# Attention sums in a fused conv, attention and expert kernel: both key blocks multiplied with the ones on TensorE, in place of one product of their GpSimd sum

## The reference

```python
dots = jnp.einsum('bhid,bhjd->bhij', q, k) * scale
attn = jax.nn.softmax(dots, axis=-1)
out = jnp.einsum('bhij,bhjd->bhid', attn, v)
```

## Time and profile before

| | |
|---|---|
| median of 3 runs | 1380.11 us |
| the profiled execution | 1380.82 us, its span 1378.8 us |
| TensorE matmul, busy in the span | 1135.6 us (82%) |
| VectorE | 827.9 us (60%) |
| ScalarE | 627.5 us (46%) |
| GpSimd | 573.8 us (42%) |
| L626, GpSimd's additions | 128 of 2360 ns |
| L1117, the products with the ones | 1024 passes, 83.5 us busy |

### The profile page before, as it was taken

One profiled execution on the slowest core, in us unless ns is written; L12 is line 12 of the kernel. 1 busy time (PEld: TensorE's weight loads), 2 busy tenths in 40 slices (PEclk: granted clock), 3 DMA queues, 4 the chain that ended last, 5 costly groups with the idle time before them and its releaser, 6 DMA issues.

```text
span 1378.8 us, 29094 instructions
## 1 busy us (share of the span) xinstructions
PE 1135.6 (82%) x10071; PEld 739.4 (54%) x10071; DVE 827.9 (60%) x1478; ACT 627.5 (46%) x1113; POOL 573.8 (42%) x437
## 2 busy tenths in 40 slices
PE   3989897966699989897987992149999999999943
PEld 2444444433244544453444442139899999998732
DVE  1556554665688768877787664525555555555545
ACT  0646455643477568557655761023333333333411
POOL 1414132333388658688877885221111221112100
PEclk9999999987699989999999997569999999999975
DMA  3124293635032221322324122921111121111258
GB/s 106 62 94 166 77 391 110 196 90 179 16 75 73 73 71 50 111 78 79 89 80 116 33 70 74 369 83 47 48 47 47 47 58 51 48 47 44 67 161 308
DMA packets 96376, 138.93 MB, mean 101 GB/s; under 512 B 18152, under 2 KB 71464, under 8 KB 95496
## 3 DMA queue, kind: packets, MB, share of 16 engines
q1 hardware_dynamic: 85032, 94.39, 22.9%
q0 software_dynamic: 11232, 42.94, 8.8%
HBM read 83.55 MB, written 53.56 MB: 99 GB/s over the span
## 4 chain that ended last, share of the span: by engine, by line
PE 65%; DVE 13%; DMA 6%; issue 5%; POOL 3%; ACT 3%; DVEq 2%; SPq 2%; PEldq 0%; ACTq 0%; POOLq 0%; PEld 0%
PE PP L894 22%; PE PP L1234 13%; PE PP L1109 7%; PE PP L1128 6%; DVE mxp L1430 5%; PE PP L962 3%; PE PP L1117 3%; PE PP L1050 3%; PE PP L928 3%; PE PP L1008 3%; POOL list_d L658 2%; DMA list_d<-WORK,idx 1%; PE PP L1207 1%; DVEq L1435 1%; DMA WORK<-in_L_ffn_W_dram 1%
## 5 line engine op out<-in xcount | busy, mean ns | idle before, releaser
L1430 DVE TENSOR_REDUCE mxp<-PP 128x2 f32<-128x1024 f32 x256 | 301.2, 1218 | 87.0 <-PE PP L1050 86.6
L834 ACT ACTIVATE WB<-PP 128x512 f32<-128x512 f32 x512 | 269.6, 604 | 175.2 <-PE PP L1128 174.6
L626 POOL TENSOR_TENSOR WB<-WB 128x1024 f32<-128x1024 f32 x128 | 301.5, 2360 | 105.8 <-PE PP L1117 95.2
L866 ACT ACTIVATE WORK<-PP,b1c 128x256 f32<-128x256 f32 (+1 forms) x320 | 143.7, 450 | 257.4 <-PE PP L894 253.9
L709 POOL DMA_INDIRECT y_d<-WORK,place x71 | 73.1, 1030 | 347.0 <-DVE WORK L1758 337.5
L894 PE MATMUL PP<-WORK,WB 128*128 128x256 f16 (+1 forms) x1920 | 208.0, 264 | 3.1 <-DVE WORK L1733 3.0
L1234 PE MATMUL PP<-WB,WORK 128*128 x1704 | 193.9, 273 | 0.0
L894 PEld LDWEIGHTS PP<-WORK,WB 128*128 x1920 | 176.8, 99 | 29.5 <-issue 4.0
L1128 PE MATMUL PP<-WORK 97*128 97x256 f16 x1024 | 162.5, 283 | 23.8 <-ACT WB L834 20.0
L1234 PEld LDWEIGHTS PP<-WB,WORK 128*128 128x128 f16 x1704 | 164.5, 98 | 21.0 <-issue 0.4
L605 POOL TENSOR_TENSOR WB<-WORK,WB 128x1024 f16<-128x1024 f32 x32 | 67.9, 2122 | 222.1 <-ACT WORK L746 222.0
(11 more groups left out here) (236 smaller groups left out, 1097.9 us busy)
## 6 DMA issues: line engine op xcount, KB each, us to landing
WORK<-in_L_ffn_W_dram POOLq DMA_DIRECT2D x32, 512.0 KB, 4.2
WORK<-list_d SPq DMA_DIRECT2D x32, 258.0 KB, 2.9
res_d<-WORK SPq DMA_DIRECT2D x8, 1024.0 KB, 4.6
WB<-late_d SPq DMA_DIRECT2D x4, 2048.0 KB, 15.9
WORK<-y_d SPq DMA_DIRECT2D x16, 512.0 KB, 8.8
WORK<-in_x_dram SPq DMA_DIRECT2D x8, 512.0 KB, 4.0
v_d<-WORK SPq DMA_DIRECT2D x4, 1024.0 KB, 5.4
WORK<-q_hi_d SPq DMA_DIRECT2D x16, 256.0 KB, 3.8
```

Source lines behind the costliest of these rows:

```text
L626: pool.tensor_tensor(PS[n % 2], PR[n % 3][:, 0], PR[n % 3][:, 1], ALU.add).then_inc(s("pair_kept"), 1)
L834: act.activation(PR[n % 3][:, c // 2, c % 2 * 2:c % 2 * 2 + 2], SCORES[m % 3] .rearrange("p (h n) -> p h n", h=2), ACT.Exp).then_inc(s("e_ ...
L866: act.activation(hid[u][:, k, 0:width], hidden_bank(k)[:, 0:width], ACT.Gelu, bias=b1c[:, bass.ds(e, 1), k], scale=1.0 / WSCALE)\
L1430: dve.tensor_reduce(mxp[:, n // 4 % 2, i, h:h + 2, k], PP[2 + h // 2][:, :].rearrange("p (h n) -> p h n", h=2), X_AXIS, ALU.max).then_inc( ...
```

## The change

The GpSimd no longer adds the two key blocks, and the buffers `PS` and the semaphore `pair_kept` are gone. In their place `sum_heads` multiplies each of the two blocks' exponentials with the ones, in 8 float32 products and so 16 passes a step, which accumulate in the same place. It needs no wait of its own, since `weigh_heads` just ahead of it has waited for the same exponentials. GpSimd keeps the wait for `pv_made` at the head of each step of its loop.

```diff
-        PS = [WB[:, e].bitcast(F32)[:, 12 * QN:16 * QN].rearrange("p (h n) -> p h n", h=GH) for e in (E - 3, E - 4)]
...
-            def add_pair(n):
-
-                pool.wait_ge(s("e_kept"), 4 * n + 4)
-                if n >= 2:
-                    pool.wait_ge(s("pv_made"), FREE + n - 1)
-                pool.tensor_tensor(PS[n % 2], PR[n % 3][:, 0], PR[n % 3][:, 1], ALU.add).then_inc(s("pair_kept"), 1)
...
             for n in range(B * STEPS):
                 b, t = n // STEPS, n % STEPS
-                add_pair(n)
+                pool.wait_ge(s("pv_made"), FREE + n - 1) if n >= 2 else None
...
-                pe.wait_ge(s("pair_kept"), n + 1)
-                for h in range(GH):
-                    mm = pe.matmul(WEIGHED[h * D:(h + 1) * D, QN:2 * QN], onesf[:, :], PS[n % 2][:, h],
-                                   start=False, stop=(n % 4 == 3), skip_group_check=True)
+                for i in range(2):
+                    for h in range(GH):
+                        mm = pe.matmul(WEIGHED[h * D:(h + 1) * D, QN:2 * QN], onesf[:, :], PR[n % 3][:, i, h],
+                                       start=False, stop=(n % 4 == 3 and i == 1), skip_group_check=True)
```

More of the change, by code:

```diff
@@ L289, in hybrid_block @@
                      "ld_stage0 ld_stage1 scaled split_hi split_lo st_last wts_split "
-                     "ld_g0 ld_g1 ld_m0 ld_m1 sum_kept rin_kept rstd_kept ld_nm mx_made mx_kept pair_kept ld_sum inv_kept st_inv ld_inv0 ld_inv1 st_made e_kept pv_made nrm_kept "
+                     "ld_g0 ld_g1 ld_m0 ld_m1 sum_kept rin_kept rstd_kept ld_nm mx_made mx_kept ld_sum inv_kept st_inv ld_inv0 ld_inv1 st_made e_kept pv_made nrm_kept "
                      "c_made c_kept nm_kept nmT_made nmr_kept ld_wo ld_res0 pr_made stat1_kept "
```

## The result

The kernel with eight products and no additions takes 1396.69 us (median of 4 runs, 1394.09 to 1398.96), the kernel before, measured beside it, 1380.4 (4 runs, 1378.25 to 1381.34). The ratio is 1.0120, 95% interval 1.0108 to 1.0133: slower by 1.2%, or 16.3 us. The forecast was 1408.0, or 27.2 more than before. The sign and the range held; the forecast loss was too large by 11 us.

The account below looks back on a forecast made before the run. The prediction took TensorE to bound attention's plain steps (2.90 us). Added passes cost 41.1 us, removed additions give back 13.9, net +27.2 on the profiled 1380.8 us: 1408.0 us, range 1391 to 1420.

Parts of the forecast that it names:

- the price of a step: Attention steps with TensorE on the path: eight added passes cost 0.445 us, between bounds of nothing and 0.61.
- The faster rival: Attention's plain steps: VectorE's loop sets 2.90 us, added passes fit into TensorE's waits; 1367 us, chance 0.05.
- what VectorE gets back: Choice of experts, t = 26 to 31: without additions 19.45 us falls to 17.3, 2.2 each in batches 1 and 2.
- the scatters: t = 17, batches 2 and 3: without additions GpSimd's scatters keep up and ScalarE need not wait; 3.4 us each won.
- The two at t = 9 and 10 vanish in the wait of 2.87.: Batches 1 to 3: TensorE's wait at t = 10 covers both steps' added sums, leaving 1.98 us of it.
- I take the difference, 0.5 us each.: t = 10, batches 2 and 3: gain from L1333 no longer holding ScalarE, 17.07 against 16.52 us, 1.0 together.
- The next two steps run at 1.2 GHz ... so they pay double.: Batches 1 to 3, the two steps after t = 10: added sums at the low clock cost 1.8 us a batch.
- the clock stays up: Rival at t = 10: shorter wait keeps TensorE's clock, 6.0 us won in each of three batches; 1390 us, chance 0.15.
- the 1.7 us for the clock at t = 0: Batch 2, t = 0: wait of 1.81 us falls to about 1.4, so the clock holds and 1.7 us is won.
- Steps with a turned row: Batch 0, 7 steps: TensorE's idle 0.17 us covers part of 0.445, so 0.27 each, 1.9 us together.
- The two sums at t = 4 and 5: Batches 1 to 3: the 0.68 us wait before the turned row takes all but 0.2 of their 0.89 us.
- those at t = 20, 21, 24 and 25: Batches 1 to 3: VectorE's copy is late by about 0.70 us, which covers all of the added sums.

Follow-up runs that it names:

- e1: Kernel before with the eight products but GpSimd's additions kept and still waited for: 1410.25 us, ratio 1.0252.
- e2: Kernel before without the additions, only the first key block's four products (output wrong): 1362.76 us, ratio 0.9888.
- e3: Kernel after with ScalarE's square root and what follows it one step later (t = 11): 1389.04 us, ratio 1.0080 to the kernel before.
- e11: Kernel before, unchanged, executed once more for another trace: 1381.48 us.
- e12: Kernel after, unchanged, executed once more for another trace: 1399.07 us.
- e5: Kernel before with the change made only at t = 8, 9 and 10 of batches 1 to 3: 1371.54 us, ratio 0.9933.
- e8: Kernel before, change only at t = 8 to 10 (batches 1 to 3), 15, 16 (2, 3), 26 to 30 (1, 2): 1372.50 us, ratio 0.9946.
- e9: Kernel before, change at t = 8 to 11 (batches 1 to 3), 26 to 31 (1, 2), 0, 14 to 16 (2, 3): 1368.56 us, ratio 0.9910.
- e10: Kernel before with the change at the same 32 steps as e9, and the square root one step later: 1358.24 us, ratio 0.9844.
- e4: Kernel before with ScalarE's square root and what follows it one step later (t = 11): 1369.86 us, ratio 0.9938.
- e7: Kernel before with the change made only at t = 26 to 30 of batches 1 and 2: 1379.11 us, ratio 0.9995.

## Why the prediction was right in sign and too high in size

The terms of its sum, with what the two profiles show (us):

| term | forecast | measured |
|---|---|---|
| up to the first sums | 0 | +1.2 |
| batch 0 | +11.2 | +12.1 |
| t = 9 to 12, three batches | +4.4 | -7.8 |
| t = 27 to 31, batches 1 and 2 | -4.4 | -4.1 |
| t = 17 and 18, batches 2 and 3 | -5.4 | -5.9 |
| all other steps of batches 1 to 3 | +20.2 | +21.2 |
| the stage's end | +1.2 | +1.0 |
| attention | +27.2 | +17.8 |
| the stages behind it | 0 | -2.3 |

The rows are rounded. Forecasts are net of added and removed parts of a term; "all other steps" is the rest of the 16.8 us up to the last unit but one, and "the stage's end" what the last normalisation moved beyond them. The last row is from one trace of each; what makes it was not looked into.

**Right: the price of a step.** 0.43 us measured, 0.445 forecast, and TensorE on the path in batch 0 and in the steps named. The faster rival (VectorE's loop as the real bound) is gone: the 73 us stretch stayed full and the step grew by all of it.

**Right: what VectorE gets back,** 2.05 us in each of two batches against 2.2, down to the durations of 225 and 171 ns.

**Right in size, one cause too few: the scatters.** 2.9 and 3.0 us a batch net, 2.7 forecast. But e1 shows that either half of the change ends that wait, so it was not the removal's gain alone.

**Wrong: the step at t = 10.** It was forecast 12.2 us too dear, while attention as a whole was 9.4 too dear; the small terms went the other way. Three readings failed in it.

- "The two at t = 9 and 10 vanish in the wait of 2.87." They could not. The sums at t = 9 stand ahead of the scores of t = 10, whose exponentials come ahead of ScalarE's table loads, so they move the whole wait back. The sums at t = 10 stand behind the wait (L1120 at 518.66, L1109 at 519.92 in batch 1). The wait is measured from TensorE's own work, through ScalarE and VectorE, and is 2.74 us with four products (e2) or eight. So all four steps pay 0.43, as they would anywhere.
- "I take the difference, 0.5 us each." The removal took the wait in batches 2 and 3 from 5.15 to 2.74, so 2.4 us each, as the length of L1333 had said. I had set the two batches' lengths beside each other, 17.07 and 16.52, and read the small difference as the price of the longer wait. The lower clock of batch 1, 0.69 against 0.80, had hidden that price; I noted the clock and did not take it out.
- "The next two steps run at 1.2 GHz ... so they pay double." I took batch 1's clock for all three batches and left it there in the kernel after. It rose instead, which is the rival "the clock stays up" in part. The result, 1396.7, lies nearer that rival's 1390 than the forecast's 1408. The rival's price has the same fault: it takes the 5.1 us of batch 1 three times, where batch 2 had lost 0.20 x 17.07 = 3.4.

With these three put right the stretch comes out. t = 9 to 12 by batch, as the wait's change, the four sums, and half of the change in time at 1.2 GHz: batch 1 -0.13 + 1.73 - 3.3 = -1.7 (measured -1.74); batch 2 -2.42 + 1.73 - 1.8 = -2.5 (-2.30); batch 3 -2.41 + 1.73 - 3.5 = -4.2 (-3.73). Of the miss of 12.2, the waits are 4.0 (-5.0 in place of -1.0), the sums themselves 0.2 (5.2 in place of 5.4, which had two at double price and two at nothing), and what remains, 8.0, goes with the clock.

The same sum fits e3 against the kernel after (wait -1.19 each; lengths -1.1, -2.8 and -1.2) but is off by about 1 us in one batch of e2 and in one of e1. That the waits and the clock make the difference is shown by these runs; that nothing else does is not.

**Right by luck: the 1.7 us for the clock at t = 0.** The prediction read the earlier trace rows as if the wait of 1.81 us took the clock away. The same trace has 1.81 us at t = 0 of batch 3 with the clock at 1.00 throughout. Over all traces here the clock fell behind 7 of 11 waits of 1.75 to 1.82 us at this place, and behind none of 10 waits of 1.17 to 1.59 us. So the shorter wait (1.18 in after) did win something, one fall in two seams, about the size forecast, but not for the reason that was read from the rows.

**Small ones.** Steps with a turned row paid 0.43 where 0.27 was forecast: the 0.17 us that TensorE waits there is for VectorE's copy of a row that TensorE itself has just made, and so moves with it. The two sums at t = 4 and 5 paid 0.05 (0.2 forecast), and those at t = 20, 21, 24 and 25 paid 0.15 to 0.25 in most places (nothing forecast). These waits are for work that VectorE does behind its own queue, and they do shrink.

**What stays open: why the clock held.** The Trainium skill (TensorE: Matmul & The Clock Gate, Part 1) says that the phase of the monitor is free, so that equal programs may see different outcomes at one place; e11 and e12 agree, by 22.97 against 21.30 and 21.67 against 20.12 us. Beyond that the runs show this: with waits of 2.87 and 5.15 us, 20.0 to 24.2 us at 1.2 GHz over three batches; with 2.74 us three times, 16.6 (e2), 7.0 and 7.0 (after, twice), 6.8 (e5), 10.1 (e8) and 10.4 (e9); with 1.26 to 1.54 us, none (e10); with 1.55, 3.3 (e3). One wait of 1.07 us (batch 1 of e4) had 3.4 all the same. e1 has 17.3 with waits of 3.61, 4.86 and 4.85 us. Shorter waits go with less low clock and so do fuller steps around them, but e9 and the kernel after, with the wait left at its place, kept 10.4 and 7.0. No run changed the wait alone with the work around it fixed and often enough to say more.

## What to carry to other kernels

Before a wait is counted as cover for added work, follow it back to where it starts: if it starts in the same engine's earlier work, it moves with that work and covers nothing. Take the granted clock out of two lengths before their difference is read as the price of something else. And an operation that frees one engine and loads the bound one is worth it only at the steps where the freed engine is late: here 32 of 128 steps made -0.9% (e9) of what was +1.2% over all 128, and -1.6% with the square root one step later (e10), which alone made -0.6% (e4).

## What the runs showed of the hardware that was not expected

- A small VectorE operation can be drawn out to the end of a GpSimd addition even with one input: a copy of 128x8 took 1.99 us (e7) where 0.17 is its own time, a tensor-scalar operation of 128x8 took 2.60 and 2.62 where 172 ns is its own. L1333 had begun 0.2 us ahead of the addition, so to be first did not spare it. Not every one is held: a reciprocal of 128x8 took 0.19 us within an addition (e7, 573.85). The reductions from PSUM show no stretch in the mean (1218 and 1219 ns). With the additions gone at one place and kept at the next, the collision only moved (e7, batch 1 to 2: -2.5 at t = 27 to 31, +2.9 at t = 0 and 1).
- A lagging engine can be cured by slowing the others. The two steps at which ScalarE had to wait for GpSimd's scatters took 9.90 us when a plain step took 2.90, and 7.13 when it took 3.33 (e1), with the same scatters and additions.
- Over the whole of attention TensorE spent some 37 us at 1.2 GHz in both traces of before (clock 0.96 over 465 us), and some 10 and 19 in the two of after (0.99 and 0.98 over 482 and 484), each good to 5 us only, while the times of after differed by 2.7 us between them.
